# Split latents in the rounded type, one bank for the jobs and three for the maxima, in a fused FFN, latent-attention and FFN block

## What is computed

```python
x = x + 0.5 * ffn(layernorm(x))     # base x@W.T + b, and 8 experts of rank 16, of which the top 2 are gated
x = x + attn(layernorm(x))
x = x + 0.5 * ffn(layernorm(x))

# attn: 16 heads, 16 content + 32 rotary features per head, values of 16
kv_c = x @ W_kv                     # 64 latents, RMS-normalised, times g_kv
q_c  = x @ W_q                      # 128
k_content, v = heads(kv_c @ W_kdec), heads(kv_c @ W_vdec)
q_content    = heads(q_c @ W_qdec)
k_rope, q_rope = rope(x @ W_krope), rope(q_c @ W_qrope)
attn = softmax(causal(q @ k.T / sqrt(48)));  out = (attn @ v) @ W_o
```

## Time and profile before

| what | us |
|---|---|
| three runs | 2002.25, 2007.97, 2008.69 |
| median | 2007.97 |
| the profiled execution, its own time | 2005.28 |
| its span in the trace | 2002.8 |

### The profile page before, as it was taken

The page is one execution under the profiler, slowest core; times in us unless marked ns, Lnnn a source line. Parts: engine busy times, 40 slices in busy tenths (PEclk is TensorE's granted clock), DMA queues, the critical chain, the costliest instruction groups (busy, mean ns, idle before and its releaser), DMA issues.

```text
span 2002.8 us, 32215 instructions
## 1 busy us (share of the span) xinstructions
PE 1901.2 (95%) x10832; PEld 1325.5 (66%) x10832; DVE 1439.5 (72%) x4555; ACT 1024.3 (51%) x2125; POOL 849.4 (42%) x912
## 2 busy tenths in 40 slices
PE   6789999999999999999999999999999999999995
PEld 5446766666677666766677667666767667677554
DVE  5767777777776877778777777788777687677632
ACT  3436554555454554545555545555556455454450
POOL 3446453553433635255441644435453454422121
PEclk9979999999999999999999999999999999999997
DMA  3687666676665666676566576646677566665511
GB/s 101 191 207 173 169 153 173 163 173 152 174 157 123 175 159 162 164 168 162 152 155 162 145 196 161 167 115 171 168 166 196 129 172 160 159 155 122 116 33 45
DMA packets 169812, 307.58 MB, mean 154 GB/s; under 512 B 15088, under 2 KB 33776, under 8 KB 169648
## 3 DMA queue, kind: packets, MB, share of 16 engines
q1 hardware_dynamic: 169648, 305.53, 61.0%
HBM read 179.12 MB, written 126.35 MB: 153 GB/s over the span
## 4 chain that ended last, share of the span: by engine, by line
PE 68%; DMA 10%; DVE 8%; POOL 7%; ACT 2%; issue 2%; SPq 1%; POOLq 0%; DVEq 0%; ACTq 0%
PE st_b L755 12%; PE o_b L775 11%; PE mx_b L787 11%; PE st_b L757 10%; PE tp_b L824 4%; PE wj_b L712 4%; DMA st<-k_scratch 3%; PE tp_b L821 3%; PE wj_b L681 2%; PE wj_b L714 2%; DMA q_scratch<-lo_t 2%; PE wj_b L699 2%; DVE xn L1077 2%; PE wj_b L692 2%; DVE mx_b L977 1%
## 5 line engine op out<-in xcount | busy, mean ns | idle before, releaser
L859 ACT ACTIVATE probs<-st_b 128x512 f32<-128x512 f32 (+3 forms) x1536 | 708.3, 489 | 537.9 <-PE st_b L757 504.4
L977 DVE CUSTOM_DVE_ANT_0 mx_b<-mx_b,tri 128x256 f32<-128x256 f32 (+3 forms) x1024 | 511.0, 515 | 141.2 <-PE mx_b L787 136.9
L755 PE MATMUL st_b<-st 97*128 97x512 f32 (+2 forms) x1536 | 588.2, 387 | 10.6 <-ACT probs L859 6.8
L787 PE MATMUL mx_b<-st 96*128 96x256 f32 (+2 forms) x1536 | 565.5, 411 | 12.4 <-DVE mx_s L980 6.3
L757 PE MATMUL st_b<-st,k_st 96*128 96x512 f32 (+2 forms) x1536 | 533.4, 351 | 0.0
L1169 POOL TENSOR_SCALAR_AFFINE_SELECT probs<-probs 128x512 f32<-128x512 f32 x256 | 168.2, 660 | 607.9 <-ACT probs L859 607.5
L980 DVE TENSOR_REDUCE mx_s<-mx_b 128x1 f32<-128x512 f32 (+1 forms) x512 | 333.2, 651 | 117.0 <-PE mx_b L787 110.4
L787 PEld LDWEIGHTS mx_b<-st 96*128 96x128 f32 x1536 | 282.0, 191 | 169.6 <-issue 80.1
L755 PEld LDWEIGHTS st_b<-st 97*128 97x128 f32 x1536 | 293.1, 191 | 134.7 <-issue 61.4
L757 PEld LDWEIGHTS st_b<-st,k_st 96*128 96x128 f32 x1536 | 294.9, 192 | 33.0 <-issue 9.8
L775 PE MATMUL o_b<-probs,v_s 128*17 128x512 f32 (+3 forms) x3072 | 285.7, 490 | 2.0 <-POOL probs L1169 1.9
(11 more groups left out here) (189 smaller groups left out, 2302.7 us busy)
## 6 DMA issues: line engine op xcount, KB each, us to landing
st<-q_scratch SPq DMA_DIRECT2D x128, 384.0 KB, 5.9
st<-k_scratch SPq DMA_DIRECT2D x128, 384.0 KB, 8.7
k_st<-k_scratch SPq DMA_DIRECT2D x128, 384.0 KB, 10.4
q_scratch<-hi_t SPq DMA_DIRECT2D x32, 768.0 KB, 3.8
q_scratch<-lo_t SPq DMA_DIRECT2D x32, 768.0 KB, 5.2
k_scratch<-hi_t SPq DMA_DIRECT2D x30, 768.0 KB, 4.3
k_scratch<-lo_t SPq DMA_DIRECT2D x30, 768.0 KB, 4.6
ao_scratch<-o_f SPq DMA_DIRECT2D x256, 32.0 KB, 1.8
```

What stands on the lines that cost most here:

```text
L755: nc.tensor.matmul(dst, k1_st[u][0:SHIFT + 1, a, P * j:P * j + P], q_st[u][0:SHIFT + 1, a, q0:q0 + w], start=True, stop=False)
L787: nc.tensor.matmul(mx_b[:, m % 2, 0:w], q_st[u][0:SHIFT, a, P * i:P * i + P], k1_st[u][0:SHIFT, a, k0:k0 + w], start=True, stop=True).then ...
L859: nc.scalar.activation(probs[:, a, PLACE[s]:PLACE[s] + n], st_b[:, a % 2, HALF - n:HALF], ACT.Exp, scale=SCALE).then_inc(exp_done, 1)
L977: nc.vector.tensor_tensor_reduce(src, src, tri[:, HALF - n:HALF], 1.0, NEG, ALU.add, ALU.max, dst).then_inc(mx_done, 1)
```

## The change

1. **The latents and their weights are split.** kvs becomes float32r: its rows 0 to 63 hold the latents rounded (written by ScalarE's copy of kvt), rows 64 to 127 the remainder, made by a new VectorE step kv_lo. Two weight tiles replace wk_s and wkv_s: kv_hl holds the rounded weights over their remainders, kv_lh the remainders over the rounded ones. A key's piece 2 and each value product are now two accumulating float32r products. fold_g makes the two tiles. wkv_raw, cos_s and sin_s use space of hi_t and lo_t.
2. **Banks.** mx_b has three banks in place of two; wj_b has one in place of two, and lane 1 uses o_b alone. A job step waits for the step right before it.
3. **Orders.** All five strings are new, made for longer load times.

```diff
-LAT_DVE = [("stats", 1, 0), ..., ("norm", 1, 1), ("ss",), ("kvn",)]
+LAT_DVE = [("stats", 1, 0), ..., ("norm", 1, 1), ("ss",), ("kvn",), ("kv_lo",)]
...
-        wkv_s = sb("wkv_s", [P, NQ, 2 * HQ * DC])
+        kv_w = [sb(name, [P, 2, H * DC], F32R) for name in ("kv_hl", "kv_lh")]
...
-        mx_b = bank("mx_b", 2)
+        mx_b = bank("mx_b", 3)
...
-        wj_b = bank("wj_b", 2)
-        lanes = [Lane(sb, [wj_b[:, 0, :], wj_b[:, 1, :]], sb("stg", [P, GT, STGW]), sb("kvs", [P, GT, P]), ""),
-                 Lane(carve, [o_b[:, 0, :], st_b[:, 1, :]], probs[:, :, late:late + STGW],
-                      probs[:, :, late + STGW:late + STGW + P], "_2")]
+        wj_b = bank("wj_b")
+        lanes = [Lane(sb, [wj_b[:, 0, :]], sb("stg", [P, GT, STGW]), sb("kvs", [P, GT, P], F32R), ""),
+                 Lane(carve, [o_b[:, 0, :]], probs[:, :, late:late + STGW],
+                      sb("kvs_2", [P, GT, P], F32R), "_2")]
...
-                if name == "wo0" and use:
+                if use:
                     pe.wait_ge(own.wj_free, use)
-                elif use > 1:
-                    pe.wait_ge(own.wj_free, use - 1)
...
-                    if NM * g + m > 1:
-                        pe.wait_ge(mx_done, NM * g + m - 1)
-                    nc.tensor.matmul(mx_b[:, m % 2, 0:w], q_st[u][0:SHIFT, a, P * i:P * i + P],
+                    if NM * g + m > 2:
+                        pe.wait_ge(mx_done, NM * g + m - 2)
+                    nc.tensor.matmul(mx_b[:, (NM * g + m) % 3, 0:w], q_st[u][0:SHIFT, a, P * i:P * i + P],
...
-                        last = nc.tensor.matmul(dst, wk_s[:, eight], own.kvs[:, :, :], start=True, stop=True)
+                        for kk in range(2):
+                            last = nc.tensor.matmul(dst, kv_w[kk][:, 0, eight], own.kvs[:, :, :], start=(kk == 0),
+                                                    stop=(kk == 1))
...
                     for k in range(2):
-                        last = nc.tensor.matmul(tp_b[:, 0, D * k:D * k + D].rearrange("p (q n) -> p q n", q=NQ),
-                                                own.kvs[:, 2 * tt + k, :], wkv_s[:, :, HQ * DC:2 * HQ * DC],
-                                                start=True, stop=True)
+                        for kk in range(2):
+                            last = nc.tensor.matmul(tp_b[:, 0, D * k:D * k + D], own.kvs[:, 2 * tt + k, :],
+                                                    kv_w[kk][:, 1, :], start=(kk == 0), stop=(kk == 1))
...
-                    nc.scalar.activation(dst, src, fn).then_inc(own.wj_free, 1)
+                    nc.scalar.activation(dst, src, fn).then_inc(own.kv_hi if what == "kvt" else own.wj_free, 1)
...
+                    nc.vector.tensor_scalar(wkv_raw, wkv_raw, g_s[:, 0:1], None, ALU.mult).then_inc(folded, 1)
...
+                    nc.vector.tensor_copy(hl[0], both).then_inc(folded, 1)
+                    dve.wait_ge(folded, 2)
+                    nc.vector.tensor_tensor(hl[1], both, hl[0].bitcast(F32), ALU.subtract)
+                    nc.vector.tensor_tensor(lh[0], both, hl[0].bitcast(F32), ALU.subtract)
+                    nc.vector.tensor_copy(lh[1], hl[0].bitcast(F32)).then_inc(folded, 1)
+                elif name == "kv_lo":
+                    dve.wait_ge(own.kv_hi, count(g, 1) + 1)
+                    nc.vector.tensor_tensor(own.kvs[KR:P, :, :], wj_of(g, "kvt")[0:KR, :].rearrange("p (t n) -> p t n", n=P),
+                                            own.kvs[0:KR, :, :].bitcast(F32), ALU.subtract).then_inc(own.wj_free, 1)
```

Of the PE's string the first lines and the last, and the first line of ScalarE's, as they were and as they are:

```diff
-        "JJJJPPPjjPjjJJJjjjJJJJPjjPjPJjPPPPJJPJJPjPPJPJXXJXXPXXPXXPXXPXXPXXPXJXJFPXXXXPXXXXXXXPXXSSXPXXSSXXSXSXSX"
+        "JJJJPPPPjjjjJJJjjjJJJPJPjPjJjPjPPPPJPjJPJPJPPXXXPXXXPXXXPXXXPXXXPXPFPJJPXXXJXXXPSSXXSXPXXSXSXXSXSXXSXSXS"
...
-        "SXSSXSSXXFSVXSXSXSXSXSXSXSXSXVXXSSXXSSXXSSXXSSXVXXSSXXSSXXSSXSXSXSVXXSSSSFSSSVSSSSSSSSSVSSSSSSSVSSSSSSSS"
-        "VSSJJSSSSSSVSSJJSSJJSSSSSVSSSSJSJJVjjjjjjjjj",
+        "SSSSSSVSSSJSSJSSSVSSSSSJSSJSSJSSVJSSSVJJJjjjjjjjjj",
...
-        "BJJJJwwwwwCJCCjjCjjJjjJJJJCjjCjCJjCHCCHCJJCJJCjJCHCJCHCCCCCBCCHCCEEECEEEEEHEECEECEECEEHCEECEECJEEJEEHJEE"
+        "BJJJwwwwwJCCCCjJjjjJjjJJJCJCjCjJjCjHCCHCCJCjJCJCHCJHCCCCJCCCBHJCCCEEEEEHEEEEEECEECEEECHCCCEEEEEEEEEEHEEE"
```

More of the change, by code:

```diff
@@ L150 @@
[L150 to L154, removed]
@@ L419, in build @@
         wq_raw, wkr_raw = raw[:, 0:H * DQ], raw[:, H * DQ:H * DQ + KD * H * DR].rearrange("p (k n) -> p k n", k=KD)
+        wkv_raw = hl_t[0][0][0:KR, 2, :].bitcast(F32)
+        cos_s, sin_s = [hl_t[0][1][:, 2, TB * DR * i:TB * DR * (i + 1)].bitcast(F32).rearrange("p (k c) -> p k c", c=DR)
+                        for i in range(2)]
         wide = [part[:, 0:2, :].rearrange("p a t -> p (a t)").bitcast(F32) for part in hl_t[0]]
@@ L510, in wj_of @@
         def wj_of(n, name):
-            return lanes[LANE[n]].banks[bank_use(n, name) % 2]
+            return lanes[LANE[n]].banks[0]
         def last_use(m):
@@ L705, in job @@
                 elif name in ("y0", "y1"):
-                    if k == 0:
-                        pe.wait_ge(own.wj_free, bank_use(n, "gated_tr") + 1)
                     for tt in range(2):
@@ L717, in job @@
                         pe.wait_ge(w2_in, 16 * N_W2)
-                    pe.wait_ge(own.wj_free, bank_use(n, "tr21") + 1)
                     nx = own.stg
@@ L812, in _ @@
                         pe.wait_ge(sorted_w, 5)
-                    if g == 1 and k == 2:
-                        pe.wait_ge(folded, 2)
+                        pe.wait_ge(folded, 3)
                     if pair == 0:
@@ L959, in _ @@
                 nc.vector.memset(own.kvn[:, :, :], 0.0)
-            for tile in mxf:
-                nc.vector.memset(tile[:, :], 0.0)
-            nc.vector.memset(wkv_s[KR:P, :, :], 0.0)
-            nc.vector.memset(wk_s[KR:P, :], 0.0)
-            nc.vector.memset(lanes[0].kvs[KR:P, :, :], 0.0)
-            nc.vector.memset(lanes[1].kvs[KR:P, :, :], 0.0).then_inc(const, 1)
+            nc.vector.memset(mxf[1][:, :], 0.0)
+            nc.vector.memset(mxf[0][:, :], 0.0).then_inc(const, 1)
             dve.wait_ge(const, CONST)
@@ L973, in _ @@
                     dve.wait_ge(mx_full, NM * g + m + 1)
-                    src = mx_b[:, m % 2, 0:n]
+                    src = mx_b[:, (NM * g + m) % 3, 0:n]
                     dst = mx_s[:, HQ * HT * (i // HT) + HT * a + i % HT, c:c + 1]
@@ L1061, in _ @@
                     dve.wait_ge(w2_in, 16 * N_W2)
[L1062 to L1066 removed]
+                    nc.vector.tensor_scalar(wkv_raw, wkv_raw, g_s[:, 0:1], None, ALU.mult).then_inc(folded, 1)
+                    dve.wait_ge(folded, 1)
+                    both = wkv_raw.rearrange("p (q x n) -> p x q n", q=NQ, x=2)
+                    hl, lh = [[w[rows, :, :].rearrange("p x (q n) -> p x q n", q=NQ) for rows in (slice(0, KR), slice(KR, P))]
+                              for w in kv_w]
+                    nc.vector.tensor_copy(hl[0], both).then_inc(folded, 1)
[7 more added lines that the diff above has]
+                                            own.kvs[0:KR, :, :].bitcast(F32), ALU.subtract).then_inc(own.wj_free, 1)
                 elif name == "widen":
```

178 lines of the change are left out of this document (67 added, 111 removed).

## The result

| | us |
|---|---|
| kernel before, median of 5 (range) | 2006.95 (2002.25 to 2008.69) |
| changed kernel, median of 5 (range) | 1976.42 (1974.01 to 1990.35) |
| ratio, 95% interval | 0.9863 [0.9831, 0.9896] |
| profiled execution of the changed kernel, its span | 1990.35, 1988.6 |

The change saves 30 us, and the forecast was 1974. The changed kernel was measured three more times for the experiments, each time beside the kernel before on the same chip: 0.9940 [0.9913, 0.9966], 0.9874 [0.9845, 0.9903] and 0.9894 [0.9872, 0.9917]. The gain is there in all four sets, between 12 and 30 us, and it differs between them by more than each interval says.

A forecast was written before the change was run, and what follows sets the result against it. The prediction took the middle as bound by the PE's own work, the ends not. Terms -23 + 1 + 3 - 15 - 8 + 10 + 3 - 2 = -31, loads -1, gave -32: 1974 us, forecast 1955 to 1984 (chance 0.48), range 1948 to 2010.

The forecast's parts named there:

- The rounded products: Key pieces and value products in the rounded type: 25.6 us less PE work, taken as -23 us.
- rival 4: The rounded products run at the pace of float32 instructions, 1997 us; chance 0.02.
- all but about one in eight of these lie in the PE-bound middle: Key pieces and value steps: most savings count fully, those in the first 100 us fall among waits; hence -23 of 25.6 us.
- kv_lo: VectorE's 16 new subtractions for the latents' remainders, which the order can hide: +1 us, bounds 0 and +11.
- The head: Kernel start: weights' split in fold_g, some +2.5 us on VectorE, and low1's copy behind the sorts, some 3 us later: +3 us.
- The third bank: Maxima: a product may be three ahead of its reduction, holding one VectorE burst more: -15 us, at most 57.8 us of waits.
- The scores' spacing: More PE work between a score and the one after next, so less waiting for exponentials: -8 us, between -19 and 0.
- One bank for a job's steps: Each job step waits until its predecessor's bank is emptied: +10 us, or 55 us in the middle if copies come late.
- rival 3: Late copies at lane 0's single bank and late shift rows make the kernel slower, 2040 us; chance 0.11.
- Shift rows and loads: Scores wait for later shift rows, +3 us (bounds 0 and 64); more room for quad loads, -1 us.
- The tail: Kernel end: job 30's steps moved behind the last V, -5 us; last job on one bank, +3.6 us; together -2 us.
- most of this fits in: Tail: 5.7 us of job 30's work fits into the 9.58 us idle after the last V: -5 us.

The follow-up runs named there:

- e_after2: The changed kernel with no edit, measured again beside the kernel before: 1977.88 us, 0.9874 of the kernel before.
- e_new_lane1: The changed kernel with lane 1's second bank back: 1975.33 us, 0.9855 of the kernel before.
- e_after: The changed kernel with no edit, measured again on another chip: 1991.09 us, 0.9940 of the kernel before.
- e_new_nobias: The changed kernel with GpSimd's bias additions cut from 256 to two columns: 1983.09 us, 0.9888 of the kernel before.
- e_new_f32: The changed kernel with keys and values in plain float32 again and no kv_lo: 2000.17 us, 0.9983 of the kernel before.

## Why the prediction was right, and where it was not

Idle time, from the starts as above, by stretch and by the tile that was late (before, then e_after2; the third stretch is shorter after the change):

| stretch | all | st_b | mx_b | wj_b | tp_b | lane 1 |
|---|---|---|---|---|---|---|
| up to 200 us | 41.9, 51.3 | 1.8, 2.5 | 7.5, 4.3 | 6.6, 11.3 | 22.8, 27.3 | 1.2, 4.8 |
| 200 to 1850 | 124.3, 116.5 | 46.2, 41.1 | 31.2, 33.0 | 17.5, 18.4 | 10.4, 5.0 | 0, 0 |
| behind 1850 | 42.9, 38.1 | 15.1, 12.5 | 2.4, 0.0 | 1.9, 6.7 | 0.2, 0.0 | 21.8, 16.7 |

**The rounded products: -23, found -18.** Paces and work are as predicted, 0.23 and 0.12 us and 25.1 us of work; rival 4 is out. The step "all but about one in eight of these lie in the PE-bound middle" took the middle for wholly bound. Its records are 98% busy, but by the starts 124 us there were idle already, and 7 us of the saved work turned into such waits in the new order, 22 us in the old one. In the medians of one chip only 9 to 12 us are left; the clock of the changed kernel was lower there (0.973 against 0.978).

**kv_lo: +1, found 0.** Its other bound, 11 us, was met, in the ratios at least, in the order that was not made for it.

**The head: +3, found between 2 and 6.** The first maxima start at 90.9 us, where it was 85.2; up to 200 us the idle time grew by 9 us, and a higher clock gave back 3 to 7. My reason for it was not borne out: with low1's copy moved ahead nothing was gained.

**The third bank: -15, found +2 in the middle and -4 in all.** This is the term that was mis-sized most. I priced the bank as slack over the old order: the same pairs, with one burst more of room. But the text itself counted 262 runs of three or more in the new order, and these use the room up at once; the waits became fewer and longer, 48 us where I wanted 35. Of the 33 us of idle time at mx_b in the middle, some 10 stand in one place of the order, met five times with 2.0 us each (last section). The bank is worth 300 us to the new order. That it would be worth little as slack under the old one is not shown, since no run tried that. What the runs of three buy is the next term.

**The scores' spacing: -8, found -5 in the middle and -7 in all.** The named wait went from 45.7 to 33.5 us. There is a gain beside it for which I had no term: tp_b, through which all pieces pass, makes the PE wait 5 us less in the middle, I take it because more work lies between two of its uses.

**One bank for a job's steps: +10, found +10 in all, but +1 in the middle.** The steps there have other work between them, and rival 3 did not come: L668 waits 0.4 us for its copy in 22 places, where that rival needed 55 us. The other 9 are in the head and the tail, where I had booked them a second time under other names. Of the 4.8 in the tail 3.4 are no bank's cost: there gated_tr waits for its gates from GpSimd, as the tail's rows below show. So at wj_b the single bank cost some 6 us, and lane 1's came on top (3.6 us of idle time in the head, 4.2 us in the tail by e_new_lane1). The rule of the Trainium skill (Perfetto Trace Analysis, Matmuls), that independent groups should rotate through banks, is borne out by the last job: there nothing else lies between the steps, each waits 0.49 to 0.85 us, and with the second bank the job from wo0 on is 4.2 us shorter. In the middle products of other tiles take the place of the rotation.

**Shift rows and loads: +3 and -1, found +2 and 0.** The weight loads and products of the scores wait 2.3 + 1.5 us for the shift row, where it was 1.0 + 0.5; in e_after2 it is 1.1 + 0.9, so +2 is the upper end.

**The tail: -2, found +2.5.** From the start of the last V to the end it was 45.2 us and is 53.4, less the 5.7 us of work that stood ahead of that V. The profiled execution had a lower clock there; in three later traces it is 51.8 to 51.9, and the term comes to +1. The last job on one bank cost what I said: 3.6 us said, 4.2 found. The step that failed is "most of this fits in": gated_tr, y0 and y1 do not run through but wait on their own chain. Timeline of the changed kernel:

```profile
1935.21 0.84 PE L729 MATMUL o_b<-probs,v_s 128*17 128x256 f32 x16 [1.07 <-POOL probs L1129]
1939.26 1.09 PE L662 MATMUL wj_b<-ident,xn 128*128 128x128 f32 x4 [3.20 <-POOL xn L1157]
1941.03 2.07 PE L668 MATMUL wj_b<-w_s,xt 128*128 128x256 f32 x4 [0.69 <-ACT xn L906]
...
1950.06 1.24 PE L639 MATMUL o_b<-wo_s,probs 128*128 128x256 f32 x5
```

wo0 starts 14.9 us behind that V, and did so 10.4 us behind it when it waited for the load alone. The cover was 4.4 us too short.

**The sum: -32, found -30.** In the traces of before and of e_after2 it is work -25.1 (said: -23), idle time -3.2 (said: -9) and the lower clock -1.6 (not said). In the middle the waits sum to -8, where my terms for it came to -10, though hardly one of them was right: the third bank was 17 us too large, the single bank 9, and tp_b's 5 were missing. So the total was met in part because errors of both signs stood in it, and that the first set came within 3 us of 1974 is luck too: the same kernel had a median of 1991 in another set, outside the forecast's 1955 to 1984, at a lower clock, for which the sum has no term.

## What to carry to other kernels

An order and its banks are one design: price a buffer together with the order that uses it, since the third bank was worth 300 us to the order made for it, and the 15 us that I had reckoned for it as slack over the old order were not found. Work taken off the busiest engine gave 18 us of 25 in an order made anew and some 4 in the old one, where loads and reductions came no earlier; after such a cut make the order anew, with the loads' times in it. For a step that runs alone at the end of a kernel give each group a bank of its own.

## What the runs showed of the hardware

**A short stop, and a granted clock that fell behind it.** The profiled execution was 14 us above the median, and the clock accounts for it: 43.5 us against 30.0 in the table. One such fall, windows of the changed kernel (stretch, length, busy PE, PEld, DVE, ACT, POOL, granted clock, DMA share, GB/s) and then the same stretch of e_after:

```profile
797.00:803.00 6.00, 4.72 (x30) 2.16 (x28) 5.99 (x20) 2.69 (x8) 5.25 (x9) 1.00 1.04 249
803.00:813.00 10.00, 9.34 (x45) 4.65 (x46) 6.17 (x28) 1.19 (x2) 1.06 (x1) 0.51 0.88 172
```

```profile
803.00:813.00 10.00, 9.74 (x70) 7.04 (x71) 9.23 (x41) 3.99 (x8) 1.78 (x3) 1.00 1.05 253
```

At 1.2 GHz the PE gets 45 matmuls done in 10 us and not 70. Ahead of it stands this, timeline of the changed kernel:

```profile
797.03 2.82 POOL L1152 TENSOR_TENSOR xa<-xa,hb_s 128x256 f32<-128x256 f32 x4
...
798.49 3.18 DVE L1054 TENSOR_TENSOR ls<-hl,m 128x32 f32<-128x32 f32 x1
...
799.80 1.82 POOL L1129 TENSOR_SCALAR_AFFINE_SELECT probs<-probs 128x512 f32<-128x512 f32 x3
801.66 0.68 DVE L931 TENSOR_REDUCE mx_s<-mx_b 128x1 f32<-128x512 f32 x1
...
802.39 0.39 PE L741 MATMUL mx_b<-st 96*128 96x256 f32 x1 [1.05 <-DVE mx_s L931]
```

A subtraction of 32 columns took 3.18 us on VectorE and ended when GpSimd's seven instructions in a row did; the reduction behind it came late, the PE stopped, and the clock fell at 803.2 us. At 1040.13 us the subtraction took 3.18 us again, and the clock fell at 1045.6. In seven other traces of the new orders the longest of its 30 occurrences took 1.0 us (1.09 and 2.29 in the two kernels with two banks for the maxima), and with the bias additions cut the median fell from 0.35 to 0.19 and the longest to 0.71. The Trainium skill (SBUF — State Buffer, Who interferes with whom) says that a VectorE instruction with two SBUF inputs, as this one has, contends with a GpSimd instruction that reads SBUF; this trace agrees. The bias additions cost nothing in the mean that can be measured (e_new_nobias was no faster), but here two such stops were each followed by a stretch at half clock. A stop does not decide it: of the nine falls between 200 and 1850 us in this trace the other seven came behind other stops, of 1.5 to 3.1 us between two starts, and behind stops of 2.49 us at 681.3 and 1391.7 us the clock stayed up.

**The same contention in a place that comes back.** GpSimd's rotary products (L484 to L489, 1.3 us each) stood beside the small instructions of the gates, which have two inputs each. Timeline of e_after2:

```profile
1141.59 1.31 DVE L1063 TENSOR_TENSOR k2m<-iota,ixf 128x32 f32<-128x32 f32 x1
...
1142.94 1.20 DVE L1068 TENSOR_TENSOR msk<-k1m,k2m 128x32 f32<-128x32 f32 x1
...
1144.27 1.10 DVE L1072 TENSOR_TENSOR em<-ex,msk 128x32 f32<-128x32 f32 x1
...
1145.62 1.05 DVE L1078 SCALAR_TENSOR_TENSOR den<-se,sm 128x4 f32<-128x4 f32 x1
...
1147.00 0.88 PE L741 MATMUL mx_b<-st 96*128 96x256 f32 x3 [2.01 <-DVE mx_s L928]
```

The last three have medians of 0.16 to 0.19 us in this trace. The reductions of the maxima stood behind them, and the PE waited 2.0 us. The same wait stands in this trace at 681, 913, 1147, 1383 and 1615 us and as often in the profiled execution. In e_after, e_new_f32 and e_new_nobias four or five of the five are only 1.25 us long, and the kernel before has no such place. That is 6 to 10 us of the idle time at mx_b; whether another place in VectorE's string gives them back was not tried.

**The clock is part of the price of a change.** The kernel before ran at 0.979 to 0.980 in the mean of every set, the changed one at 0.973 to 0.977. One fall of 10 us at 1.2 GHz loses some 5 us, more than the stop of 1 to 2 us ahead of it. Why the changed kernel has more of them, and why one chip had more than the other, stays open: no run took the stops away, and e_new_nobias left the rotary products where they were.
